# A two-layer graph network on one core: the second self weight's magnitudes are read early, and LayerNorm's row statistics move to other instructions

## The reference

```python
def _sage_layer(h, edge_src, edge_dst, deg_inv, W_self, W_neigh, b):
    msg = h[edge_src]
    agg = jax.ops.segment_sum(msg, edge_dst, num_segments=h.shape[0])
    mean = agg * deg_inv[:, None]
    return h @ W_self + mean @ W_neigh + b

deg_inv = 1.0 / jnp.maximum(deg, 1.0)
h = jax.nn.relu(_sage_layer(x, edge_src, edge_dst, deg_inv, W_self0, W_neigh0, b0))
out = _sage_layer(h, edge_src, edge_dst, deg_inv, W_self1, W_neigh1, b1)
y = x + out
return (y - mean(y)) / sqrt(var(y) + 1e-5)      # per row
```

## Time and profile before

| | us |
|---|---|
| median of 3 runs (lowest, highest) | 699.4 (699.3, 701.48) |
| the profiled execution, its own time | 701.54 |
| its span in the trace | 699.9 |
| PE busy | 635.0 (91%) |
| DVE busy | 497.0 (71%) |
| ACT busy | 274.1 (39%) |
| POOL busy | 117.6 (17%) |

### The profile page before, as it was taken

One profiled execution on the slowest core, in us unless ns is written; L12 is line 12 of the kernel. 1 busy time (PEld: TensorE's weight loads), 2 busy tenths in 40 slices (PEclk: granted clock), 3 DMA queues, 4 the chain that ended last, 5 costly groups with the idle time before them and its releaser, 6 DMA issues.

```text
span 699.9 us, 11077 instructions
## 1 busy us (share of the span) xinstructions
PE 635.0 (91%) x3286; PEld 325.6 (47%) x3286; DVE 497.0 (71%) x1209; ACT 274.1 (39%) x492; POOL 117.6 (17%) x200
## 2 busy tenths in 40 slices
PE   3688989998999999999998999999979879879795
PEld 3644545544666666555554444444434334333242
DVE  7796487868777875398999866632029996676764
ACT  5572734343334344036444544423215331222221
POOL 3001236533233333100000000002121220000000
PEclk9799999999999999999999999999998989999998
DMA  8614000000000000333111000007724526100111
GB/s 316 236 63 178 1 1 0 0 1 1 0 1 1 0 0 0 117 126 120 60 60 32 0 1 1 0 1 248 264 91 150 178 86 242 61 31 30 61 60 54
DMA packets 16141, 50.33 MB, mean 72 GB/s; under 512 B 2616, under 2 KB 2776, under 8 KB 16096
## 3 DMA queue, kind: packets, MB, share of 16 engines
q1 hardware_dynamic: 16096, 49.77, 20.2%
HBM read 40.45 MB, written 9.31 MB: 71 GB/s over the span
## 4 chain that ended last, share of the span: by engine, by line
PE 58%; DVE 19%; issue 9%; DMA 5%; ACT 5%; SPq 1%; POOL 1%; DVEq 0%; POOLq 0%; ACTq 0%
PE ps L674 15%; PE ps L771 14%; PE ps L713 12%; PE ps L647 10%; PE ps L571 4%; DMA ws<-in_L_gnn_W_neigh 2%; DVE xz L1365 2%; ACT wn L966 2%; DMA wn<-in_L_gnn_W_self 2%; PE ps L808 2%; DVE table L1358 2%; DVE table L1340 2%; DVE wn L308 1%; DVE wn L1531 1%; DVE wn L1373 1%
## 5 line engine op out<-in xcount | busy, mean ns | idle before, releaser
L771 PE MATMUL ps<-xz,wn 128*128 128x512 f16 x600 | 137.3, 389 | 11.9 <-DVE ws L1531 6.2
L647 PE MATMUL ps<-wn,xz 128*128 128x512 f16 x480 | 116.4, 382 | 2.8 <-DVE wn L308 1.4
L674 PE MATMUL ps<-xz,ws 128*128 128x420 f16 (+1 forms) x576 | 116.1, 339 | 0.0
L836 ACT ACTIVATE scratch<-ps 128x240 uint16<-128x240 f32 x160 | 59.0, 371 | 120.3 <-PE ps L571 101.9
L1129 DVE TENSOR_SCALAR lohot<-iota_lo,table 125x128 f16<-125x128 f16 x320 | 87.8, 274 | 25.2 <-PE ps L571 24.6
L1131 DVE TENSOR_SCALAR scratch<-iota_q,table 125x240 f16<-125x240 f16 x320 | 104.5, 327 | 0.3 <-issue 0.2
L771 PEld LDWEIGHTS ps<-xz,wn 128*128 128x128 f16 x600 | 59.5, 100 | 87.3 <-DVE wn L1373 11.7
L485 POOL TENSOR_TENSOR A<-A,scratch 128x120 int32 x160 | 72.8, 455 | 138.9 <-ACT scratch L836 110.1
L808 PE MATMUL ps<-wn,A 128*128 128x512 f16 x200 | 79.1, 396 | 11.6 <-DVE scratch L1472 11.6
L713 PE MATMUL ps<-A,zh 128*128 128x420 f16 (+1 forms) x480 | 84.7, 340 | 0.0
L808 PE MATMUL ps<-ws,A 128*128 128x512 f16 x200 | 78.9, 394 | 0.0
(11 more groups left out here) (177 smaller groups left out, 658.4 us busy)
## 6 DMA issues: line engine op xcount, KB each, us to landing
ws<-in_L_gnn_W_neigh SPq DMA_DIRECT2D x16, 512.0 KB, 4.5
wn<-in_L_gnn_W_self SPq DMA_DIRECT2D x16, 512.0 KB, 5.0
zh<-in_x SPq DMA_DIRECT2D x9, 512.0 KB, 8.6
scratch<-in_x SPq DMA_DIRECT2D x9, 512.0 KB, 6.3
ws<-in_L_gnn_W_neigh SPq DMA_DIRECT2D x4, 1024.0 KB, 17.8
ws<-in_L_gnn_W_self SPq DMA_DIRECT2D x4, 1024.0 KB, 8.7
partial<-scratch SPq DMA_DIRECT2D x8, 512.0 KB, 3.8
wn<-partial SPq DMA_DIRECT2D x4, 512.0 KB, 6.9
```

What stands on the lines that cost most here:

```text
L647: ins = pe.matmul(ps[0:TP, 2 * r + half, :], lhs(a, k, t), w[:, k, b, half * HD:(half + 1) * HD], start=(k == 0 and a == 0 and b == 0), st ...
L674: ins = pe.matmul(ps[:, b, 0:CH[n]], ws[:, k, a, bass.ds(f * P, P)], xT[h][:, k, CO[n]:CO[n] + CH[n]], start=(k == 0 and a == 0 and h == 0 ...
L771: ins = pe.matmul(ps[:, b, :], slot[:, k, a, :], Tm[m][:, k, w, :], start=(m in (1, 2, 5) and k == 0 and a == 0 and w == 0), stop=(k == HK ...
L836: act.activation(stage[0:TP, r], ps[0:TP, 8 - banks + r % banks, 0:HN].rearrange("p (j w) -> p j w", j=JT), ACT.Copy).then_inc(counts_copi ...
```

## The change

Three things change.

1. `W_self1`'s magnitudes are read during the units. A new loader brings one block of 128 rows at a time into a buffer of its own in `ws`, ACT sums the absolute values of its two halves (`ws1_sums`, in every second unit from the fifth on), and the scale is ready before the first products. All eight blocks' magnitudes are read by it; the four turns of magnitude loads between the first products and the tiles are gone.
2. In the tiles the four steps k that prepare `W_self1` begin at tile 0 instead of tile 3, with the sums after even tiles and the low halves after odd ones. The block sums of h for the first second-stage products come after tile 7 instead of tile 8. POOL spreads the maximum before the first products, not between two bias additions.
3. In the second products the y updates that complete half a row write out the row sums as well (`accum_out`), which gives the mean. ACT computes the sum of squared deviations over the whole row (`Square` with the negative mean as bias), the root and the normalising; DVE keeps three one-column operations. The row's finish comes one product later in DVE's queue, and `item_lows` comes behind the y update. The last pair of row tiles still shares the normalising between DVE and ACT. Rows of the other pairs are stored in one transfer.

The diff, cut (declarations of semaphores and buffers left out):

```diff
+    ROW7 = {}
+    for pair in range(IT):
+        ROW7[AT7[pair, 3 if pair < IT - 1 else 2]] = 2 * pair
+        ROW7[AT7[pair, 4]] = 2 * pair + 1
...
+        def load_ws1(eng, k):
+
+            if k:
+                eng.wait_ge(ws1_summed, 2 * k)
+            eng.dma_start(ws1raw, Ws1[k * P:(k + 1) * P, :]).then_inc(ws1_in, 16)
...
                 for u in {0: (2, 3), 1: (4, 5), 3: (6,), 5: (7,)}.get(f, ()):
                     load_raw(sp, 0, u)
+                for k in {1: (1,), 2: (2, 3), 3: (4,), 4: (5,), 5: (6, 7)}.get(f, ()):
+                    load_ws1(sp, k)
...
-            for u in range(2):
+            for u in range(HK, HK + 2):
                 load_raw(sp, 1, u)
             sp.wait_ge(z_low, 4 * IT)
             for n in range(2):
                 load_x(n)
-            for u in range(2, HK):
-                load_raw(sp, 1, u)
...
-                for u in {0: (4, 5), 3: (6,), 4: (7,)}.get(n, ()):
+                for u in {1: (6,), 3: (7,)}.get(n, ()):
                     load_raw(sp, 1, u)
...
             spread(2)
+            spread(3)
...
-            for n in range(3):
-                residual(n)
-            spread(3)
-            for n in range(3, JT):
+            for n in range(JT):
                 residual(n)
...
+            def ws1_sums(k):
+
+                act.wait_ge(ws1_in, 16 * (k + 1))
+                for a in range(2):
+                    m = MC["ws1"] + 2 * k + a
+                    act.activation(ws1dump, ws1raw[:, a * HD:(a + 1) * HD], ACT.Abs,
+                                   accum_out=mx[:, m:m + 1]).then_inc(ws1_summed, 1)
+                    act.wait_ge(ws1_summed, 2 * k + a + 1)
...
+                    if q >= -2 and q % 2 == 0 and q < 2 * KT - 2:
+                        ws1_sums(q // 2 + 1)
...
             for k in range(HK):
-                weight_sums(1, k, unread)
-            act.wait_ge(scale_ready, 6)
-            for k in range(HK):
                 for i in range(ITEMS):
                     t_item(1, k, i)
...
+            def root(n):
                 p, r = n // 2, n % 2
+                act.wait_ge(mean_ready, n + 1)
+                apart(act)
+                act.activation(bank(6)[0:TP], yrow(p, r), ACT.Square, bias=st[0:TP, r, 2:3],
+                               accum_out=st[0:TP, r, 3:4]).then_inc(square_ready, 1)
+                act.wait_ge(square_ready, n + 1)
+                act.activation(ln[0:TP, r, 1:2], st[0:TP, r, 3:4], ACT.Sqrt, bias=eps[0:TP],
+                               scale=1.0 / D).then_inc(std_ready, 1)
...
-                if m == (3 if p < IT - 1 else 2):
-                    finish(2 * p)
-                if m == 4:
-                    finish(2 * p + 1)
+                if e and e - 1 in ROW7:
+                    normalize(ROW7[e - 1])
+                if e in ROW7:
+                    root(ROW7[e])
+            normalize(JT - 1)
...
+                    if (f, n) == (6, 2):
+                        dve.wait_ge(ws1_summed, 2 * KT)
+                        tensor_max("ws1", 2 * KT, MC["ws1"])
+                    if (f, n) == (7, 1):
+                        scale("ws1")
+                        signal(scale_ready)
...
-                if 3 <= n < 3 + HK:
+                if n < 2 * HK and n % 2 == 0:
                     for i in range(4):
-                        t_sum4(1, n - 3, i)
-                    t_lows(1, n - 3, range(ITEMS))
-                if n == JT - 2:
+                        t_sum4(1, n // 2, i)
+                if n < 2 * HK and n % 2 == 1:
+                    t_lows(1, n // 2, range(ITEMS))
+                if n == 2 * HK - 1:
                     dve.wait_ge(t_low, 2 * ITEMS * HK)
                     for e in range(ITEMS):
                         s_sum(1, e)
+                if n == JT - 2:
                     for e in range(ITEMS):
                         item_lows(1, e)
+            def mean(n):
...
+                dve.tensor_scalar(st[0:TP, r, 2:3], st[0:TP, r, 0:1], st[0:TP, r, 1:2], -1.0 / D,
+                                  ALU.add, ALU.mult).then_inc(mean_ready, 1)
...
-                    item_lows(1, e + ITEMS)
...
+                    dve.scalar_tensor_tensor(yh, ps[0:TP, 3 * (p % 2) + b, :], c("cs1", TP), yh, ALU.mult, ALU.add,
+                                             accum_out=st[0:TP, r, h:h + 1]).then_inc(y_acc, 1)
...
+                if e + ITEMS < NP7:
+                    item_lows(1, e + ITEMS)
+                if e and e - 1 in ROW7 and e < NP7 - 1:
+                    finish(ROW7[e - 1])
+                if e in ROW7:
+                    mean(ROW7[e])
```

More of the change, by code:

```diff
@@ L118, in gnn_kernel @@
         fl = sb("fl", [P, 8], F32)
-        st = sb("st", [P, 2, 12], F32)
-        mv = sb("mv", [P, 2, 2], F32)
+        st = sb("st", [P, 2, 4], F32)
+        eps = sb("eps", [P, 1], F32)
         ln = sb("ln", [P, 2, 4], F32)
@@ L277, in gnn_kernel @@
         t_low = sem("t_low")
+        ws1_in = sem("ws1_in")
+        ws1_summed = sem("ws1_summed")
         part_out = [sem(f"part_out{i}") for i in range(2)]
@@ L318, in load_raw @@
             slot, k = u % 2, u % HK
-            if 2 <= u < HK + 2:
-                eng.wait_ge(max_done, 2 * (HK * phase + u - 1))
+            if phase == 0 and 2 <= u < HK + 2:
+                eng.wait_ge(max_done, 2 * (u - 1))
             elif u >= HK + 2:
@@ L447, in _ @@
                 rows = min(TP, N - t * TP)
+                if p < IT - 1:
+                    sp.wait_ge(o_ready[0], n + 1)
+                    apart(sp)
+                    sp.dma_start(out[t * TP:t * TP + rows, :], yrow(p, r)[0:rows]).then_inc(o_stored[r], 16)
+                    continue
                 for h in (1, 0):
                     half = slice(h * HD, (h + 1) * HD)
-                    sp.wait_ge(o_ready[h], n + 1)
+                    sp.wait_ge(o_ready[h], r + 1 if h else n + 1)
                     apart(sp)
```

70 lines of the change are left out of this document (32 added, 38 removed).

## The result

The changed kernel takes 665.03 us (median of 4 runs, 664.67 to 666.7) against 700.44 us for the kernel before on the same chip (4 runs, 699.3 to 701.57): ratio 0.9499, 95% interval 0.9472 to 0.9526. The forecast was 666.0. The profiled execution took 664.71 us with a span of 663.0.

The account below looks back on a forecast made before the run. PE was taken to bound the kernel, losing time to waits on DVE and half clock after stalls. Span 699.9 - 17.9 - 20.8 + 2.4 + 1.4 = 665.0; with 1.6 around it 666.6, less 2.1 is 664.5, plus 1.5 is 666; range 659 to 680.

Parts of the forecast that it names:

- Tiles: Tile stage: no PE stall left and full clock back, the whole 17.9 us gained; bounds 9 and 17.9.
- Second products: Second products: DVE loses statistics, joinings and half rows, PE runs through without waiting, 20.8 us gained.
- Read-out: Second products: writing out DVE's row sum costs 0.2 us each; bounds 0 and 0.75 us.
- Units: Units: ACT's new sums and loads delay DVE, first products begin 2.4 us later; bounds 0.5 and 15.8.
- the +0.6 of the next block: Units: the block after the second, loaded and summed in front of three more high halves, delays DVE 0.6 us more.
- Tail: End of kernel: last product's end to last normalising's end takes 5.9 us instead of 4.5, so 1.4 us longer.
- A: Second products stay partly bound by DVE, each of ten rows still costing 1 us: 676 us; chance 0.10.
- B: Tiles stay held, POOL's additions delaying DVE's results and stalls bringing back half clock: 677 us; chance 0.09.
- C: Units: the early loads cost more, up to 15.8 us: 672 to 680 us; chance 0.07.
- D: Units: ACT's chain of load, sums, load makes the kernel slower than before, 702 us at 11 us landings; chance 0.02.
- E: Tiles and second products: stalls were not what clock and waits say, only one stage gains: 684 us; chance 0.04.
- for small waits at the edges: Stage edges: 1.5 us added to the sum of 664.5 us for small waits, giving 666.

## Why the prediction was right, and where it was not

- **Tiles, -17.9 forecast, -17.6 measured.** DVE, POOL and SP all kept up as worked out. A low half on DVE beside a POOL addition still takes long (496.82: 2.83 us for 0.74), and one tile result waited 5.6 us for POOL at 512.38, and none of this reached PE. The cause was named only in part: POOL's two gaps, with which the prediction explained the late DVE, are worth 4.8 us by themselves; the load of x behind the loads that wait for ACT's sums, which the prediction did not name, another 4.8.
- **Second products, -20.8 forecast, -20.6 measured, with the causes weighed wrongly.** The prediction named the wait of 0.76 us in front of the update among the reasons why DVE is late, and of the change it said that "the trip to ACT for a low half now lies behind the update"; but it gave this no price and let the removed passes of DVE carry the gain. Its bound was PE's own time, which gave the right number whatever the cause: that the total came out is no evidence for its account, and in that much it is luck. The runs show the order as the larger part: 16.8 us of 19.0 alone, and the whole new LayerNorm without it 7.6. The row [0.76 <- ACT] in the earlier trace rows stood 19 times in that stage, 14.2 us. With DVE's busy time of 75.75 us that makes 90.0, as much as PE's 90.5 for the stage, so DVE had nothing to spare; I counted engine time (13.7 of 18.1 us for the changed kernel) and no waits. The total of the waits is not their price, though: 32.3 us with the low half ahead cost 11.4 us of the stage, and 9.5 us behind the update cost nothing. What counts is whether an update stands behind the wait.
- **Read-out.** 0.2 us assumed from ACT's 0.19, 0.08 measured. That it is an instruction of its own with no inputs is what the Trainium skill says (VectorE: DVE Perf Modes, section Two Vector instructions with no wait between them); the trace agrees: its row names 128x1 written and no shape read, and lasts 0.08 us.
- **Units, +2.4 forecast, +2.7 measured in one profile and +1.3 in the other.** Composed otherwise: the first wait was to be 2.0 us at the high half; it came as 0.99 at the relu and 1.24 (0.53 in the other profile) behind the slow landing of 5.6 us, as the issue at 320.31 and the sums at 325.94 show; the +0.6 of the next block did not come, since later loads landed in a median of 3.6 us. The scale (379.51 to 380.24) stands where DVE had waited 1.26 us for PE; of that wait nothing is left, and the 0.15 us at 380.39 are DVE's wait for its own scale.
- **Tail, +1.4 forecast, +0.7 measured** to the last normalising (5.2 us after the last matmul instead of 5.9): the last update began 1.24 us after the last matmul instead of 1.5, and of the other terms the update and the Square, each with its read-out, were 0.2 us shorter and reciprocal and shift 0.1. The span's end, behind a store, came 0.6 later.
- **Rivals.** A did not come. That its 676 is also the time with the low half ahead (676.25) is chance: A put 1 us on each of ten rows and did not name the order. B, C and D did not come either, C and D with landings of 3.6 us in the median. E did not: both stages gain, each also without the other. (By D's own cycle, landings of 11 us would have given 704, not the 702 that stands there.)
- The last 1.5 us "for small waits at the edges" were not needed; 664.5 was the sum, and 665.0 the median.

## What to carry to other kernels

When a chain of in-order instructions has a wait for another engine, ask first what stands behind it: an instruction for which the critical engine waits belongs ahead of it, if it doesn't depend on it, and then its own duration may fill the wait. Such a move is two lines and was worth 16.8 us of the stage here, where taking 17 us of busy time from DVE without it was worth 7.6. Where a sum is capped by another engine's time, a right total says nothing of which part brought it: try the parts in all combinations. And new work for an engine with slack cost most here at its first two instances, where the data wasn't there yet and other work of that engine stood close; sent earlier, it cost nothing.

## What the runs showed of the hardware

- DVE's row sum from a two-input pass costs 0.08 us (ACT's 0.18 to 0.19), and the pass is not longer with it: 0.75 us for 512 columns both in L1575 (with) and L1578 (without). The next instruction of DVE starts at the same time as the read-out (DVE timeline, changed kernel):

```profile
603.30 0.08 DVE L1575 DVE_READ_ACCUMULATOR ws<-ps,S,ws 128x1 f32 x1
603.30 0.69 DVE L1408 TENSOR_TENSOR wn<-zh,wn 128x512 f16<-128x512 f32 x1
```

- POOL lost time before and after a reduction over partitions that stood between elementwise additions: 5.80 and 7.18 us before the change, 6.11 and 7.64 in the run that put it back. In front of memsets (373.12, 373.76) no such gap stands behind it. What the engine does in these gaps no run shows.
- ACT loads a table once in this stage, at the first row's root (579.60 to 580.88), between the Square and the root:

```profile
L1065 ACT ACT_TABLE_LOAD x1 | 1.3, 1283 | 0.0
```

  Square, root, Copy and Identity then alternate for nine rows with no further load.
- The tiles of the kernel before, with their code unchanged, lasted 103.9, 100.2 and 101.6 us in three programs: this stage, held up by waits, varied by some 4 us. In the second PE's waits were 8.8 us instead of 11.6; in the third they were 11.7, but the mean granted clock was 0.97 instead of 0.93. The new tiles, without waits, last 86.33 to 86.35 us in all eight profiles that have them.
